# Opening of a fused two-layer kernel: expert mixing as stacked 32-row products, x earlier in the load queue, low rank B split later, int32 conversions regrouped

## The chip, the cores and the metric

The kernel runs on one core of a Trainium2 chip. Its time is the device time of one execution in microseconds (us), lower is better. Engines: PE is TensorE, DVE VectorE, ACT ScalarE, POOL GpSimd, SP the engine that issues most DMAs.

## What is computed

The input x has 64 batches of 32 rows of 512 values, 2048 tokens. Cut to what the change touches:

```python
def cond(x, embedding, W0, b0, W1, b1, W2, b2, weight, bias_k):
    h = gelu(embedding @ W0 + b0)
    h = gelu(h @ W1 + b1)
    att = softmax(h @ W2 + b2)                      # 64 batches x 8 experts
    agg_w = einsum('bk,koi->boi', att, weight)      # a 32x32 matrix for each batch
    agg_b = att @ bias_k                            # 32 values for each batch
    return einsum('boi,bih->boh', agg_w, x) + agg_b[:, :, None]

def qlinear(x, q, scale, A, B):                     # q: integers 0 to 15
    return x @ ((q - 7.5) * (scale * 0.005)[:, None]).T + 0.02 * (x @ A @ B)

def ffn(x):                                         # 512 -> 1376 -> 512
    h = silu(qlinear(x, gate)) * qlinear(x, up)
    return qlinear(h, down)

x = x + ffn(cond(x, ...))
x = x + ffn_fp8(conv_cond(x, ...))
```

## The kernel before, in words

The 2048 tokens go through the first layer in four tiles (t = 0 to 3) of 512 tokens, a tile being four groups of 128. The second layer follows after the last tile. Each engine has one instruction stream of its own, written out in order in a block (`@block.sync`, `@block.tensor`, `@block.scalar`, `@block.gpsimd`, `@block.vector`), and the streams meet by semaphores: an instruction's `then_inc` raises one, `wait_ge` stops the engine until it has a value. A DMA raises its semaphore by 16 when it has landed. What stands behind a wait on an engine's stream stands still with it.

**The opening.** SP (L403 to L440) issues the loads in order: the packed condition inputs, the expert matrices `cond_w`, `bias_k`, the identity, `lr_a`, `lr_b`, slot 0 of the quantised weights, x of tile 0, slots 1 to 3, small scales and masks. PE runs three small layers (L519, L522, L525) with dummy bf16 matmuls between (`keep_clock`, L513; `WARM` says how many at each place). DVE and ACT make the softmax; PE waits for `soft` and for `lr_in` at 2 x 16 (the identity and `lr_a` both raise it) and transposes `att` (L529). DVE copies it as `att_t` (L1026). PE then mixes: eight fp32 products of 8 rows (L535), each 128 x 64, into bank 5, with one dummy matmul in the middle. The bias product `ones.T @ att_bias` has its operand split into an fp32r high part (ACT, L813) and a low part (DVE, L1040) and is two fp32r matmuls (L542, L543); four dummy matmuls follow. ACT (L821) and DVE (L1047) copy the mixed 32 x 32 matrices into the block-diagonal tensor `mix`.

**The condition stage.** `condition(t)` (L553) multiplies x by `mix`, 16 fp32 products of 128 x 128 in a tile, two instructions each. For tile 0 it waits for `mix_ready` and x. DVE adds `agg_b` (L1058), ACT and DVE split the result into an fp32r high part (L826) and a low part (L1068), and PE begins the tile's stream with the low rank products with `lr_a_w` (L681) and the gate and up products (L616).

**Low rank B.** ACT (L816) and POOL (L985) split `lr_b`; SP stores the parts to DRAM (L427), loads slots 4 and 5, loads the parts back in another layout into `lr_b4` (L433), then goes on with further slots. PE first needs `lr_b4` in L626.

**Gate, up and down.** The 1376 hidden units are 11 chunks (ic = 0 to 10) of 128 (the last 96). For each chunk PE makes gate and up (L616, L626), ACT scales (L921, L924), DVE adds the low rank parts (L1245, L1248), ACT applies Silu (L935), DVE multiplies (L1256), ACT and POOL split the product into `h_hi` (L893) and `h_lo` (L995). Then come four down groups j = 0 to 3 (L605), 11 chunks of four matmuls; group 0 of tile 0 waits at each chunk for `h_lo_ready` and for that chunk's converted weights.

**Conversions.** The quantised weights come as int32 in 33 slots of a ring of eight (gate and up of each chunk, then 11 for down). DVE's `convert` (L1053) makes each an fp32r weight; a slot's load waits until the conversion eight before it is done. Six are converted early. In tile 0 each chunk has two, between L1248 and L1256, so slots 6 to 27; the last five (28 to 32) come in a row after the product of chunk 10:

```python
if t == 0:
    for later in range(EARLY + 2 * ic, EARLY + 2 * ic + 2):
        convert(later)
...
if t == 0:
    for later in range(EARLY + 2 * IC, 3 * IC):
        convert(later)
```

## Time and profile before

| | before |
|---|---|
| median of 3 runs | 382.48 us |
| lowest and highest run | 381.16, 382.75 us |
| the profiled execution, its own time | 383.76 us |
| its span, first to last instruction | 382.0 us |
| granted TensorE clock, mean of the span | 0.987 |
| PE busy | 372.2 us, 97% |
| DVE busy | 249.0 us, 65% |
| ACT busy | 172.6 us, 45% |
| POOL busy | 82.3 us, 22% |
| DMA, mean rate | 106 GB/s |

The span is the profiled execution's; the rest of its time lies ahead of the first and behind the last instruction. Start times in all rows count from the first instruction. Matmuls are pipelined, so a row's duration overlaps with the next one's; the pitch is the difference of starts, which the chain of waits shows as the time of each piece. A clock of 1.00 is TensorE's full 2.4 GHz, 0.50 is 1.2 GHz.

### The profile page before, as it was taken

The page shows a single profiled execution, that of the slowest core. Times are in us where ns is not written, and L with a number is a line of the kernel's source. Part 1 is how long each engine was busy: PE and PEld are TensorE (multiplying, and loading weights), DVE is VectorE, ACT ScalarE, POOL GpSimd, SP SyncE. Part 2 cuts the span into 40 slices and gives each one's busy share as a digit, 9 for nine tenths or more (in the row PEclk, how much of TensorE's full clock was granted, in tenths as well). Part 3 has the DMA queues.
Part 4 walks back from the last instruction along what each step waited for, and adds up shares of the span by engine and source line. Part 5 has one row for each costly group of instructions (what it writes and reads, how often), then busy time and mean ns, then how long its engine had stood idle before and what let it go on. Part 6 is the DMA issues. An engine that isn't in the chain of part 4 may idle for free.

```text
span 382.0 us, 5806 instructions
## 1 busy us (share of the span) xinstructions
PE 372.2 (97%) x2233; PEld 307.9 (81%) x2234; DVE 249.0 (65%) x406; ACT 172.6 (45%) x323; POOL 82.3 (22%) x68
## 2 busy tenths in 40 slices
PE   8999999899999999999999999999999999999894
PEld 3877887799888888998888889988888899995341
DVE  2659999826376665263766652638889722797994
ACT  6546798313355554133555541335666510254132
POOL 2101433411123224111233241112332411000000
PEclk9699999999999999999999999999999999999998
DMA  6897575198420000232200002354000399965235
GB/s 208 276 275 238 154 270 161 56 319 184 60 43 0 0 2 0 34 51 42 41 0 3 1 0 33 52 79 112 2 0 2 115 280 233 197 184 92 90 133 222
DMA packets 81964, 40.53 MB, mean 106 GB/s; under 512 B 52344, under 2 KB 72840, under 8 KB 81808
## 3 DMA queue, kind: packets, MB, share of 16 engines
q1 hardware_dynamic: 69280, 37.80, 37.4%
q10 hardware_dynamic: 12480, 1.56, 2.9%
q0 software_dynamic: 176, 0.79, 0.6%
q8 instruction: 18, 0.29, 0.3%
q14 instruction: 10, 0.08, 0.1%
HBM read 26.38 MB, written 13.75 MB: 105 GB/s over the span
## 4 chain that ended last, share of the span: by engine, by line
PE 92%; DVE 5%; issue 1%; DVEq 0%
PE ps L616 41%; PE ps L605 23%; PE ps L626 5%; PE ps L553 4%; PE ps L647 4%; PE ps L784 3%; PE ps L513 2%; PE ps L764 2%; PE ps L681 2%; PE ps L649 2%; DVE down_w L1053 1%; PE ps L568 1%; DVE b_buf L1248 1%; DVE q_fp L1328 1%; PE ps L535 1%
## 5 line engine op out<-in xcount | busy, mean ns | idle before, releaser
L995 POOL TENSOR_TENSOR h_lo<-a_buf,h_hi 128x512 fp32r<-128x512 f32 (+1 forms) x44 | 58.0, 1318 | 125.2 <-ACT h_hi L893 125.2
L605 PE MATMUL ps<-down_w,h_hi 128*128 128x288 f32 (+1 forms) x352 | 76.4, 298 | 1.0 <-DVE down_w L1053 1.0
L605 PE MATMUL ps<-down_w,h_lo 128*128 128x288 f32 (+1 forms) x352 | 74.8, 293 | 0.0
L616 PE MATMUL ps<-x_hi,up_w 128*128 128x512 f32 (+1 forms) x176 | 69.7, 396 | 0.2 <-DVE b_buf L1248 0.2
L616 PE MATMUL ps<-x_hi,gate_w 128*128 128x512 f32 (+1 forms) x176 | 69.9, 397 | 0.0
L616 PE MATMUL ps<-x_lo,gate_w 128*128 128x512 f32 (+1 forms) x176 | 69.4, 395 | 0.0
L616 PE MATMUL ps<-x_lo,up_w 128*128 128x512 f32 (+1 forms) x176 | 69.3, 393 | 0.0
L605 PEld LDWEIGHTS ps<-down_w,h_hi 128*128 128x128 f32 (+1 forms) x352 | 57.2, 189 | 2.6 <-POOL h_lo L995 1.2
L605 PEld LDWEIGHTS ps<-down_w,h_lo 128*128 128x128 f32 (+1 forms) x352 | 56.1, 188 | 0.0
L1256 DVE TENSOR_TENSOR a_buf<-a_buf,b_buf 128x512 f32<-128x512 f32 (+1 forms) x44 | 49.5, 1125 | 9.6 <-ACT a_buf L935 8.5
L921 ACT ACTIVATE a_buf<-ps,gate_sc 128x512 f32<-128x512 f32 (+1 forms) x44 | 30.2, 686 | 27.4 <-POOL h_lo L995 24.8
L1248 DVE TENSOR_TENSOR b_buf<-ps,b_buf 128x512 f32<-128x512 f32 (+1 forms) x44 | 30.2, 686 | 18.9 <-ACT b_buf L924 14.7
L1144 DVE TENSOR_TENSOR y_buf<-ps,y_buf 128x512 f32<-128x512 f32 x16 | 11.1, 691 | 46.7 <-PE ps L568 46.7
L924 ACT ACTIVATE b_buf<-ps,up_sc 128x512 f32<-128x512 f32 (+1 forms) x44 | 30.1, 685 | 23.7 <-PE ps L616 23.6
L1005 POOL TENSOR_TENSOR x_nat<-y_buf,x_nat 128x512 f32<-128x512 f32 x15 | 19.3, 1287 | 95.8 <-DVE y_buf L1144 95.8
L616 PEld LDWEIGHTS ps<-x_hi,up_w 128*128 128x128 f32 (+1 forms) x176 | 32.6, 185 | 8.7 <-DVE b_buf L1248 0.5
L616 PEld LDWEIGHTS ps<-x_lo,up_w 128*128 128x128 f32 (+1 forms) x176 | 32.8, 186 | 8.0
L616 PEld LDWEIGHTS ps<-x_lo,gate_w 128*128 128x128 f32 (+1 forms) x176 | 32.8, 186 | 7.8
L616 PEld LDWEIGHTS ps<-x_hi,gate_w 128*128 128x128 f32 (+1 forms) x176 | 32.6, 185 | 7.9
L1245 DVE TENSOR_TENSOR a_buf<-ps,a_buf 128x512 f32<-128x512 f32 (+1 forms) x44 | 30.3, 688 | 6.6 <-ACT a_buf L921 6.0
L893 ACT ACTIVATE h_hi<-a_buf 128x512 fp32r<-128x512 f32 (+1 forms) x44 | 27.5, 625 | 9.7 <-DVE a_buf L1256 9.7
L935 ACT ACTIVATE a_buf<-a_buf 128x512 f32<-128x512 f32 (+1 forms) x44 | 27.5, 625 | 9.6 <-DVE a_buf L1245 9.3
(179 smaller groups left out, 458.8 us busy)
## 6 DMA issues: line engine op xcount, KB each, us to landing
x_nat<-in_x SPq DMA_DIRECT2D x4, 1024.0 KB, 7.3
out<-x_nat SPq DMA_DIRECT2D x16, 256.0 KB, 2.5
turned<-x_nat SPq DMA_DIRECT2D x12, 256.0 KB, 3.2
x_nat<-in_down_q SPq DMA_DIRECT2D x11, 256.0 KB, 3.1
x_nat<-in_gate_q SPq DMA_DIRECT2D x10, 256.0 KB, 6.2
x_nat<-in_up_q SPq DMA_DIRECT2D x10, 256.0 KB, 8.2
edges<-zeros SPq DMA_DIRECT2D x4, 512.0 KB, 9.2
xt<-turned SPq DMA_DIRECT2D x6, 256.0 KB, 3.4
```

What stands on the lines that cost most here:

```text
L605: last = mm(ps[:, 4 + 2 * (j % 2) + m, 0:HALF + R], part[0:k, ic, j * P:(j + 1) * P], down_w[0:k, ic, m, :], start=first, stop=end)
L616: last = mm(ps[0:k, bank(ic, 2 * m), :], w[:, H * ic + c * k:H * ic + (c + 1) * k], part[:, c, :], start=c == 0 and part is x1_hi, stop=c ...
L626: mm(ps[0:width(ic), bank(ic, 2 * m + 1), :], lr_b4[:, m, ic * P:ic * P + width(ic)], t4[m], start=True, stop=True).then_inc(l_mm, 1)
L893: activation(h_hi[0:k, ic, :], a_buf[0:k, ic % 2, :], copy).then_inc(h_hi_ready, 1)
L921: activation(a_buf[0:k, ic % 2, :], ps[0:k, bank(ic, 0), :], copy, scale=gate_sc[0:k, ic:ic + 1]).then_inc(ag_ready, 1)
L924: activation(b_buf[0:k, ic % 2, :], ps[0:k, bank(ic, 2), :], copy, scale=up_sc[0:k, ic:ic + 1]).then_inc(au_ready, 1)
L935: activation(a_buf[0:k, ic % 2, :], a_buf[0:k, ic % 2, :], ACT.Silu).then_inc(silu_ready, 1)
L995: nc.gpsimd.tensor_tensor(h_lo[0:k, ic, :], a_buf[0:k, ic % 2, :], plain(h_hi[0:k, ic, :]), ALU.subtract).then_inc(h_lo_ready, 1)
L1005: nc.gpsimd.tensor_tensor(x_nat[:, n, :], y_buf[:, j % 2, :], x_nat[:, n, :], ALU.add).then_inc(x2_ready, 1)
L1245: v.tensor_tensor(a, ps[0:k, bank(ic, 1), :], a, ALU.add).then_inc(g_ready, 1)
L1248: v.tensor_tensor(b, ps[0:k, bank(ic, 3), :], b, ALU.add).then_inc(u_ready, 1)
L1256: v.tensor_tensor(a, a, b, ALU.mult).then_inc(h_ready, 1)
```

## The change

- **Mixing.** The expert matrices are loaded four times over, stacked on 32 rows (`cond_w`), beside a second tensor with zeros on rows 0 to 7 and 16 to 23 and the matrices on the others (`cond_w_rest`). DVE makes the fp32r high part of the first, and high times a sign column (+1, -1, +1, -1 by blocks of 8 rows) plus the second: high, low, high, low. The softmax weights are written four times next to two blocks of zeros that POOL clears; two transposes of 32 rows give them four times over, and as two blocks of zeros with two of values. ACT makes the high part from PSUM, DVE the signed sum: high, high, low, low. One fp32r product over 32 rows then has all four partial products; eight take the place of the eight fp32 products and the dummy matmul between them.
- **Bias.** One fp32 product with `ones` and `att_bias` (two instructions) takes the place of the two fp32r products and the splits before them.
- **Loads.** x of tile 0 goes ahead of `lr_a`, `lr_b` and slot 0; `bias_k` behind the identity, with a semaphore of its own.
- **Low rank B.** ACT's high part comes after its copy of `agg_b`, no longer before its copies of `mix`.
- **ACT's Silu table** is loaded after `split_mixed(0)`. **`WARM[4]`** is 2.
- **Conversions.** Chunks 0 to 5 have two, chunks 6 to 10 three (18 to 20, ..., 30 to 32), and those of chunk 10 come after its product.

The diff, without allocations of memory and names of semaphores:

```diff
 BUFS = 3
-WARM = (4, 2, 1, 6, 1)
+WARM = (4, 2, 1, 6, 2)
 LRC = R * I // P
 MIX_BANK, BIAS_BANK = 5, 4
 FIRST_BANK = (6, 3, 7, MIX_BANK)
...
-COND_WIDTHS = (B, P, P, EXPERTS, 1, 1, EXPERTS)
+COND_WIDTHS = (B, P, P, EXPERTS, 1, 1, EXPERTS, 1, 1)
+PARTS = 4
+STACKED = PARTS * EXPERTS
+SPARE = 1856
...
+        pad_gate = sb("pad_gate", [P, 2 * HC * I - 4 * (S // OB) * P], F32, early)
+        cond_w_sb = sb("cond_w_sb", [STACKED, S // OB * P], F32, early)
+        cond_w_left = sb("cond_w_left", [STACKED, S // OB * P], F32, early)
+        cond_w_hi = sb("cond_w_hi", [STACKED, S // OB * P], F32R, early)
+        cond_w_parts = sb("cond_w_parts", [STACKED, S // OB, P], F32R, early)
...
         def _(sp):
             sp.dma_start(cond_in_sb[:], cond_pack).then_inc(cond_in, 16)
-            sp.dma_start(cond_w_sb[:].rearrange("k o p -> k (o p)"), cond_w).then_inc(mixw_in, 16)
-            sp.dma_start(bias_k_sb[:], bias_k).then_inc(mixw_in, 16)
+            sp.dma_start(cond_w_sb[:], cond_w).then_inc(mixw_in, 16)
+            sp.dma_start(cond_w_left[:], cond_w_rest).then_inc(mixw_in, 16)
             sp.dma_start(ident[:], ident_in).then_inc(lr_in, 16)
+            sp.dma_start(bias_k_sb[:], bias_k).then_inc(bias_k_in, 16)
+            sp.dma_start(x_nat[:, 0:TG, :], x_tile(x, 0)).then_inc(x_in[0], 16)
             sp.dma_start(stage_lr_a[:].rearrange("p c m r -> p (c m r)"), lr_a).then_inc(lr_in, 16)
...
             sp.dma_start(stage_lr_b[:].rearrange("p m n -> p (m n)"), lr_b).then_inc(lrb_in, 16)
-            load_slot(0)
-            sp.dma_start(x_nat[:, 0:TG, :], x_tile(x, 0)).then_inc(x_in[0], 16)
-            for n in range(1, 4):
+            for n in range(4):
                 load_slot(n)
             sp.dma_start(gate_sc[:], gate_s).then_inc(scale_in, 16)
             sp.dma_start(up_sc[:], up_s).then_inc(scale_in, 16)
@@ -526,21 +534,21 @@
             keep_clock(WARM[3])
             pe.wait_ge(soft, 4)
             pe.wait_ge(lr_in, 2 * 16)
-            nc.tensor.transpose(ps[0:EXPERTS, 3, 0:B], att[:], ident[0:B, 0:B]).then_inc(att_tr, 1)
+            pe.wait_ge(att_zero, 1)
+            for at, to in ((PARTS // 2, 3), (0, 2)):
+                nc.tensor.transpose(ps[0:STACKED, to, 0:B], att[:, at:at + PARTS, :].rearrange("b n k -> b (n k)"),
+                                    ident[0:B, 0:B]).then_inc(att_tr, 1)
             keep_clock(WARM[4])
 
-            pe.wait_ge(att_ready, 1)
-            pe.wait_ge(mixw_in, 2 * 16)
+            pe.wait_ge(att_parts_ready, 1)
+            pe.wait_ge(mixw_ready, 1)
             for o in range(S // OB):
-                last = mm(ps[:, MIX_BANK, o * B:(o + 1) * B], cond_w_sb[:, o, :], att_t[:], start=True, stop=True)
-                if o == S // OB // 2 - 1:
-                    keep_clock(1)
+                last = mm(ps[:, MIX_BANK, o * B:(o + 1) * B], cond_w_parts[:, o, :], att_parts[:], start=True, stop=True)
             last.then_inc(mix_mm, 1)
 
-            pe.wait_ge(bias_hi, 2)
-            pe.wait_ge(bias_lo, 1)
-            mm(ps[:, BIAS_BANK, :], ones_r[:], att_bias_hi[:], start=True, stop=False)
-            mm(ps[:, BIAS_BANK, :], ones_r[:], att_bias_lo[:], start=False, stop=True).then_inc(aggb_mm, 1)
+            pe.wait_ge(att_ready, 2)
+            mm(ps[:, BIAS_BANK, :], ones[0:EXPERTS, :], att_bias[:].rearrange("k b s -> k (b s)"),
+               start=True, stop=True).then_inc(aggb_mm, 1)
...
@@ -805,15 +813,11 @@
             load_table(1, ACT.Exp)
             act.wait_ge(soft, 2)
             activation(probs[:], logits[:], ACT.Exp, bias=stat[:, 0:1], accum_out=stat[:, 1:2]).then_inc(exp_done, 1)
-            load_table(2, ACT.Silu)
+            act.wait_ge(att_tr, 2)
+            activation(att_hi[:], ps[0:STACKED, 3, 0:B], copy).then_inc(att_hi_ready, 1)
 
             act.wait_ge(lr_in, 2 * 16)
             activation(lr_a_w[:, :, :, 0, :], stage_lr_a[:], copy).then_inc(lra_hi, 1)
-            act.wait_ge(att_ready, 2)
-            activation(att_bias_hi[:], att_bias[:].rearrange("k b s -> k (b s)"), copy).then_inc(bias_hi, 1)
-            activation(ones_r[:], ones[0:EXPERTS, :], copy).then_inc(bias_hi, 1)
-            act.wait_ge(lrb_in, 16)
-            activation(lr_b_parts[:, :, 0, :], stage_lr_b[:], copy).then_inc(lrb_hi, 1)
             act.wait_ge(mix_mm, 1)
             act.wait_ge(mix_zero, 1)
             for q in range(2, OB):
@@ -837,9 +841,12 @@
 
             act.wait_ge(aggb_mm, 1)
             activation(agg_b[:, 0:TILE], ps[:, BIAS_BANK, :], copy).then_inc(aggb_ready, 1)
+            act.wait_ge(lrb_in, 16)
+            activation(lr_b_parts[:, :, 0, :], stage_lr_b[:], copy).then_inc(lrb_hi, 1)
             act.wait_ge(mix_ready, 2)
             activation(mix_kept[:], ps[:, MIX_BANK, :], copy).then_inc(mix_saved, 1)
             split_mixed(0)
+            load_table(2, ACT.Silu)
             act.wait_ge(sel_w_in, 16)
             activation(sel[:], stage_sel[:], copy)
             x_a_high(0)
...
         @block.gpsimd
         def _(pool):
+            nc.gpsimd.memset(att[:, 0:PARTS // 2, :], 0.0).then_inc(att_zero, 1)
             nc.gpsimd.memset(mix[:], 0.0).then_inc(mix_zero, 1)
             nc.gpsimd.memset(zeros[:], 0.0).then_inc(zero_set, 1)
             pool.wait_ge(lrb_hi, 1)
...
             v.memset(warm_ones[:], 1.0).then_inc(const_set, 1)
 
+            dve.wait_ge(mixw_in, 2 * 16)
+            v.tensor_copy(cond_w_hi[:], cond_w_sb[:]).then_inc(mixw_hi, 1)
             dve.wait_ge(cond_in, 16)
+            dve.wait_ge(mixw_hi, 1)
+            v.scalar_tensor_tensor(cond_w_parts[:].rearrange("k o p -> k (o p)"), plain(cond_w_hi[:]), w_sign,
+                                   cond_w_left[:], ALU.mult, ALU.add).then_inc(mixw_ready, 1)
+
             dve.wait_ge(logit_mm, 1)
             v.tensor_tensor(logits[:], ps[0:B, 2, 0:EXPERTS], b2_sb, ALU.add).then_inc(soft, 1)
             dve.wait_ge(soft, 1)
@@ -1021,12 +1035,16 @@
             dve.wait_ge(exp_done, 1)
             v.reciprocal(stat[:, 2:3], stat[:, 1:2]).then_inc(soft, 1)
             dve.wait_ge(soft, 3)
-            v.tensor_scalar(att[:], probs[:], stat[:, 2:3], None, ALU.mult).then_inc(soft, 1)
-            dve.wait_ge(att_tr, 1)
+            v.tensor_scalar(att[:, PARTS // 2:, :], probs[:].unsqueeze(1).to_broadcast([B, PARTS, EXPERTS]),
+                            stat[:, 2:3], None, ALU.mult).then_inc(soft, 1)
+            dve.wait_ge(att_tr, 2)
+            dve.wait_ge(att_hi_ready, 1)
+            v.scalar_tensor_tensor(att_parts[:], plain(att_hi[:]), att_sign, ps[0:STACKED, 2, 0:B], ALU.mult,
+                                   ALU.add).then_inc(att_parts_ready, 1)
             v.tensor_copy(att_t[:], ps[0:EXPERTS, 3, 0:B]).then_inc(att_ready, 1)
 
             dve.wait_ge(att_ready, 1)
-            dve.wait_ge(mixw_in, 2 * 16)
+            dve.wait_ge(bias_k_in, 16)
 
             first = TILE // S
             v.tensor_tensor(att_bias[:], att_t[:, 0:first].unsqueeze(2).to_broadcast([EXPERTS, first, S]),
@@ -1035,10 +1053,6 @@
             dve.wait_ge(lra_hi, 1)
             v.tensor_tensor(lr_a_w[:, :, :, 1, :], stage_lr_a[:], plain(lr_a_w[:, :, :, 0, :]),
                             ALU.subtract).then_inc(lra_ready, 1)
-
-            dve.wait_ge(bias_hi, 1)
-            v.tensor_tensor(att_bias_lo[:], att_bias[:].rearrange("k b s -> k (b s)"), plain(att_bias_hi[:]),
-                            ALU.subtract).then_inc(bias_lo, 1)
 
             dve.wait_ge(mix_mm, 1)
...
+
+            def convert_in_chunk(ic):
+
+                done = [EARLY + 2 * n + max(0, n - IC // 2 - 1) for n in (ic, ic + 1)]
+                for n in range(*done):
+                    convert(n)
...
                     v.tensor_tensor(b, ps[0:k, bank(ic, 3), :], b, ALU.add).then_inc(u_ready, 1)
-                    if t == 0:
-                        for later in range(EARLY + 2 * ic, EARLY + 2 * ic + 2):
-                            convert(later)
+                    if t == 0 and ic < IC - 1:
+                        convert_in_chunk(ic)
                     if t == TILES - 1 and ic == W_SPREAD - 1:
                         largest_of(w_row_mm, bank(W_SPREAD, 1), w_max, w_steps)
                     dve.wait_ge(silu_ready, n + 1)
                     dve.wait_ge(u_ready, n + 1)
                     v.tensor_tensor(a, a, b, ALU.mult).then_inc(h_ready, 1)
+                    if t == 0 and ic == IC - 1:
+                        convert_in_chunk(ic)
...
-                if t == 0:
-                    for later in range(EARLY + 2 * IC, 3 * IC):
-                        convert(later)
                 for j in range(TG):
...
+    def in_parts(values):
+
+        return np.repeat(np.array(values, np.float32), EXPERTS)[:, None]
+
+    cond_w = a(L0_cond_weight).reshape(EXPERTS, S * S)
     lr_a = np.stack([a(L0_ffn_gate_A)[order], a(L0_ffn_up_A)[order]], axis=1).reshape(HC, P, 2 * R).transpose(1, 0, 2)
     cond_pack = np.zeros((P, COND_COLS), np.float32)
     for at, w in zip(COND_AT, (a(cond_128).T, a(L0_cond_W0), a(L0_cond_W1), a(L0_cond_W2), a(L0_cond_b0)[:, None],
-                               a(L0_cond_b1)[:, None], broadcast(L0_cond_b2, B))):
+                               a(L0_cond_b1)[:, None], broadcast(L0_cond_b2, B), in_parts((1, -1, 1, -1)),
+                               in_parts((1, 1, -1, -1)))):
         cond_pack[:w.shape[0], at:at + w.shape[1]] = w
...
-        "cond_w": a(L0_cond_weight).reshape(EXPERTS, S * S), "bias_k": a(L0_cond_bias_k),
+        "cond_w": np.concatenate([cond_w] * PARTS),
+        "cond_w_rest": np.concatenate([np.zeros_like(cond_w), cond_w] * (PARTS // 2)), "bias_k": a(L0_cond_bias_k),
```

## Rows read from the trace of the kernel before

**Rows 1.** The page, engine totals: busy us, share of the span, instructions.

```profile
PE 372.2 (97%) x2233; PEld 307.9 (81%) x2234; DVE 249.0 (65%) x406; ACT 172.6 (45%) x323; POOL 82.3 (22%) x68
```

**Rows 2.** The chain of waits, 0 to 100 us: start, us, what.

```profile
5.94 1.95 PE ps L513 x6
7.89 0.15 PE ps L529
...
8.36 1.08 PE ps L535 x8
...
9.77 1.25 PE ps L535 x8
...
11.98 1.82 PE ps L513 x4
13.80 5.29 PE ps L553 x32
...
31.09 0.38 PE ps L626
...
92.29 4.21 PE ps L605 x32
```

**Rows 3.** Windows: stretch, length, PE busy us, granted clock, DMA share, GB/s.

```profile
12.00:13.80 1.80, 1.80 (x5) 0.50 0.58 185
13.80:19.10 5.30, 5.30 (x33) 0.67 0.86 266
...
88.66:92.23 3.57, 3.57 (x34) 1.00 0.22 63
```

**Rows 4.** Timeline, end of tile 0, DVE and PE: start, us, engine, line, what.

```profile
66.15 0.67 DVE L1248 TENSOR_TENSOR b_buf<-ps,b_buf 128x512 f32<-128x512 f32 x1
...
68.68 0.42 PE L605 MATMUL ps<-down_w,h_hi 128*128 128x288 f32 x2
...
71.76 0.68 DVE L1256 TENSOR_TENSOR a_buf<-a_buf,b_buf 96x512 f32<-96x512 f32 x1
...
72.36 2.85 DVE L1053 TENSOR_SCALAR down_w<-x_nat 128x512 fp32r<-128x512 int32 x5
...
76.17 0.43 PE L605 MATMUL ps<-down_w,h_hi 128*128 128x288 f32 x2
```

**Rows 5.** DMA issues: what, count, KB each, median us from issue to landing.

```profile
stage_lr_a<-in_lr_a SPq DMA_DIRECT2D x1, 128.0 KB, 2.2
...
x_nat<-in_x SPq DMA_DIRECT2D x1, 1024.0 KB, 7.9
...
x_nat<-in_up_q SPq DMA_DIRECT2D x1, 256.0 KB, 8.1
...
lr_b_rows<-lr_b_parts SPq DMA_DIRECT2D x1, 688.0 KB, 3.9
...
lr_b<-lr_b_rows SPq DMA_DIRECT2D x2, 688.0 KB, 7.1
...
x_nat<-in_x SPq DMA_DIRECT2D x1, 1024.0 KB, 6.2
```

**Rows 6.** Timeline of the opening, SP's queue, DVE and POOL.

```profile
3.75 0.43 SPq L416 DMA_DIRECT2D x_nat<-in_x  x1
...
8.32 0.68 DVE L1032 TENSOR_TENSOR att_bias<-att_t,bias_k_sb 8x512 f32<-8x512 f32 x1
...
9.16 0.42 DVE L1036 TENSOR_TENSOR lr_a_w<-stage_lr_a,lr_a_w 128x256 fp32r<-128x256 f32 x1 [0.15 <-ACT lr_a_w L811]
...
10.61 1.64 POOL L985 TENSOR_TENSOR lr_b_parts<-stage_lr_b,lr_b_parts 128x688 fp32r<-128x688 f32 x1 [7.93 <-ACT lr_b_parts L816]
...
11.05 1.75 DVE L1047 COPY mix<-ps 32x32 f32<-32x32 f32 x8 [0.67 <-PE ps L535]
```

**Rows 7.** Timeline, tile 0, POOL and DVE where they meet.

```profile
39.31 1.29 POOL L995 TENSOR_TENSOR h_lo<-a_buf,h_hi 128x512 fp32r<-128x512 f32 x1 [3.06 <-ACT h_hi L893]
...
39.79 1.36 DVE L1256 TENSOR_TENSOR a_buf<-a_buf,b_buf 128x512 f32<-128x512 f32 x1 [0.44 <-ACT a_buf L935]
```

More of the change, by code:

```diff
@@ L68, in width, with build @@
     return min(P, I - ic * P)
-def build(nc, x, cond_pack, cond_w, bias_k, gate_q, up_q, gate_s, up_s,
+def build(nc, x, cond_pack, cond_w, cond_w_rest, bias_k, gate_q, up_q, gate_s, up_s,
           lr_a, lr_b, down_q, down_s, down_a, down_b, conv_w, ctx_w, fside, ffn_w,
@@ L125, in build @@
         early = ExitStack()
-        pad_gate = sb("pad_gate", [P, 2 * HC * I], F32, early)
+        pad_gate = sb("pad_gate", [P, 2 * HC * I - 4 * (S // OB) * P], F32, early)
[3 more added lines that the diff above has]
+        cond_w_parts = sb("cond_w_parts", [STACKED, S // OB, P], F32R, early)
         cond_in_sb = sb("cond_in_sb", [P, COND_COLS], F32, early)
@@ L131, in build @@
         probs = sb("probs", [B, EXPERTS], F32, early)
-        att = sb("att", [B, EXPERTS], F32, early)
+        att = sb("att", [B, PARTS + PARTS // 2, EXPERTS], F32, early)
+        att_hi = sb("att_hi", [STACKED, B], F32R, early)
+        att_parts = sb("att_parts", [STACKED, B], F32R, early)
         att_t = sb("att_t", [EXPERTS, B], F32, early)
@@ L145, in build @@
         stage_ctx_w = sb("stage_ctx_w", [P, S], F32, early)
[L147 removed]
+        used = 4 * (COND_COLS + 2 * B + (2 + PARTS * 3 // 2) * EXPERTS + 3 * B + 6 + S + TILE + SPARE + HC * 2 * R + P
                     + GROUPS + P + S + S)
@@ L156, in build @@
         early.close()
-        cond_sb, w0_sb, w1_sb, w2_sb, b0_sb, b1_sb, b2_sb = (
+        cond_sb, w0_sb, w1_sb, w2_sb, b0_sb, b1_sb, b2_sb, w_sign, att_sign = (
             cond_in_sb[0:rows, COND_AT[n]:COND_AT[n] + COND_WIDTHS[n]]
-            for n, rows in enumerate((P, P, P, P, P, P, B)))
+            for n, rows in enumerate((P, P, P, P, P, P, B, STACKED, STACKED)))
         phase2 = ExitStack()
```

10 lines of the change are left out of this document (4 added, 6 removed).

## The prediction, made before the changed kernel ran

> **What bounds the kernel now.** I began with the page's engine totals: TensorE (PE) is busy for 372.2 of 382.0 us, so a saving must come from a stretch where PE waits, runs at the lower clock or does work that can be cut [rows 1]. The chain of waits of the first 60 us says what PE does there. At 7.89 it transposes the softmax weights, from 8.36 it mixes the expert matrices in eight fp32 products (L535, two instructions each) until 9.77 + 1.25 = 11.02, then come the two bias products (L542, L543, 0.96 us) and at 11.98 four clock-keeping matmuls (L513), and from 13.80 the first condition stage (L553, 32 instructions, 5.29 us); at 19.1 the long L681/L616 stream begins [rows 2]. No step of it is a DMA. The windows give the clock: 0.50 in 12.00 to 13.80, a mean of 0.67 in the condition stage, and the same 32 instructions take 3.57 us at clock 1.00 in the second token tile [rows 3]. So 0.50 is the 1.2 GHz level and 1.00 is the 2.4 GHz level, and the low stretch costs L553 alone 5.29 - 3.57 = 1.7 us. PE had run little but small products before the fall: L535, whose operands fill 8 rows. The other weak place is the first down product: PE starts L605 at 68.68 and its second j group at 76.17, 7.49 us for 44 instructions; at the pitch of the later ones (4.21 us for 32 in the chain, 0.132 each) these need 5.8 us. 1.65 us are therefore waits, on the last product (71.76), what is split from it, and the five conversions that DVE does in a row from 72.36 [rows 4].
>
> I name T the start of the transpose, 7.9 now, and measure the opening from it.
>
> **The change, part by part.**
>
> *SP queue: when T can come.* PE waits ahead of the transpose for lr_in at 32, that is for ident and for lr_a, and the change leaves this wait. Before, lr_a stood ahead of x, was issued some 1.4 us before it and took 2.2 us to land, so it was in at about 4.5, long before T; x was issued at 3.75 and took 7.9 us (11.65) [rows 5, 6]. Now x (1 MB) stands between ident and lr_a. SP is occupied 0.43 us by an issue [rows 6]: cond_pack 0.74, cond_w 1.19, the rest 1.6, ident 2.0, bias_k 2.4, x 2.75, lr_a 3.2. The x load of tile 2, which had the queue to itself, took 6.2 us [rows 5]; so x lands between 2.75 + 6.2 = 8.95 and 2.75 + 7.9 = 10.65. I take 9.3, near the low end, since only 0.3 MB more of small loads are ahead of it, and no quantised slot. The loads that followed x before did not overtake it: the 256 KB slot issued next, at about 4.2, took 8.1 us and landed at 12.3, 0.65 after x [rows 5]. lr_a, half as large, then lands some 0.6 after x. T moves to 9.9: **+2.0 us**, bounds 9.5 and 11.2. The Trainium skill (DMA: Bandwidth & Descriptors, Queues, rings and completion order) says that each DMA engine consumes one queue's descriptors in ring order; the landings agree. By that rule alone no part of lr_a starts before the same engine's part of x.
>
> *DVE ahead of the logits.* New there: a 32x1024 copy to fp32r and a 32x1024 scalar_tensor_tensor. The nearest rows are 512-wide: a conversion (2.85/5 = 0.57 [rows 4]) and a two-operand operation (0.68 [rows 6]); doubled, 1.1 + 1.3 = 2.4 us. Their input, two loads of 128 KB just behind the first one, I put at 4.0, so they end at 6.4. The logits left PE at 5.94 [rows 2]: 0 to 0.6 us on the softmax chain. Cost nothing, because PE waits for lr_a anyway; without that cover 0.4. The wider att (64x32) adds under 0.1, with the same cover.
>
> *From T to the first condition matmul.* Two transposes, ACT's att_hi, DVE's att_parts, each 0.3, with two clock-keeping matmuls beside them (before, transpose and copy took 0.5 until L535): PE starts mixing at T + 1.2. The mixing goes from 16 instructions and a clock-keeping one (2.66 us) to 8 of one pass. Their pitch is not in the trace: below, 0.03 us, if 64 columns go as the 288 of L605 do (0.132); above, 0.156, the second half of L535 (1.25/8). A weight load of 128 columns stands before each as in L535, so I take 0.14 near the upper end, 1.1 us: T + 2.3. The bias goes from two fp32r to two fp32 instructions of 512 columns: 4 times the 128 columns of L553, whose instruction takes 3.57/32 = 0.11 us at the high clock, so 0.9 us, and 1.7 at the low one, against 0.96 before. That is T + 4.0, and the four matmuls of keep_clock (1.82 us at the low clock) end at T + 5.8. DVE's side is shorter: att_parts until T + 0.95, att_t 0.3, att_bias 0.68, lr_a low 0.42, then the mix cells 1.75 [rows 6] give T + 4.1, hidden behind PE at the low clock. Before it was 13.8 - 7.9 = 5.9. Saving **-0.1**: what the mixing gives back goes to the longer way into it and the fp32 bias. The 32 condition instructions then start at 9.9 + 5.8 = 15.7 instead of 13.8.
>
> *The clock in the condition stage.* Of 13.80 to 19.10 about 3.5 us were at 0.50 [rows 3]: (1 - 0.67)/0.5 x 5.3. If the clock rises at the same moment (17.3), the stage has 1.6 us at half rate, 0.8 us of its 3.57, and 2.8 at the full one, 4.4 in all: -0.9. If it rises later by as much as the work is later: 0. I take -0.8. x is in at 9.3, and hides. **Opening: +2.0 - 0.1 - 0.8 = +1.1 us.**
>
> *lr_b split later.* POOL's low half of lr_b started at 10.61, right after ACT's high half, and took 1.64; SP then stored it, from 12.3 [rows 6]. The high half now follows the agg_b copy, which ends at about T + 4.7 = 14.6: 0.8 more, POOL from 15.4, the store at 17.1, 4.8 later. SP's queue behind that wait: the store, slots 4 and 5, the two lr_b loads, slots 6 and 7, the down and conv inputs and slots 8 to 11. Store and loads took 3.9 and 7.1 us (a median of two; the second some 1 us more) [rows 5], so lr_b was laid at about 12.3 + 3.9 + 1 + 8 = 25 and is now at 29 to 30, while PE asks for it at 31.1 + 1.1 [rows 2]. The slots have the same slack of 2 us or more before their product. 0, bounds 0 and +1. ACT's Silu table load now lies under PE's first L681/L616 products, where no one waits for ACT: 0.
>
> *Conversions spread.* Chunks 6 to 9 get three conversions instead of two, chunk 10 none before its product and three after. One more adds at most 2.85/5 = 0.57 to DVE; I take 0.35, as a group waits for POOL once, however long it is. Four of them make 1.4 by chunk 10 if DVE has no idle time in these chunks, 0.7 if half is absorbed, which I take. PE waits for u of chunk 9 before L605: that came at 66.15 + 0.67 = 66.8, L605 started at 68.68, 1.9 later [rows 4]: covered. Last product: before at 71.76, after two conversions; now about 71.0, where POOL's h_lo of chunk 9 runs until about 71.7. The row for such a meeting is L1256 at 39.79: 1.36 us instead of 0.68, until POOL's h_lo from 39.31 was over [rows 7]. So product 10 ends 72.35, ACT's h_hi 73.0, POOL's h_lo 74.4 to 74.7, conversions by 74.7. Unstalled, PE needs them at 68.7 + 40 x 0.132 = 74.0. Waits left 0.4 to 0.7, and I take 0.4: **-1.25 us**, bounds -0.6 and -1.65. The Trainium skill (SBUF — State Buffer, Who interferes with whom) has it that a DVE operation with both inputs in SBUF and a GpSimd one that reads there block each other; the 1.36 agrees. By the rule without a meeting the saving would be 1.65.
>
> **Sum.** The profiled execution took 383.76 us. +1.1 - 1.25 = -0.15: 383.6. It stands 1.28 above the median of the runs (382.48), so the forecast is **382.3 us**. A measurement of this kernel can't tell less than about 0.5%, 1.9 us, from no change.
>
> **The rivals.**
> 1. *lr_a does not wait for x, and the clock holds* (0.15). T is 8.0 to 8.3, PE is not idle, mixing and bias run at 1.00 and end at T + 2.6; DVE's mix cells bind, T + 4.1; condition from 12.5 to 16.1, 3.0 before 19.1. With the conversions -4.25: 378.2. For it: lr_a is small. Against: the landings behind x. If only T is early and the clock falls all the same, condition starts at 8.0 + 5.8: -1.25 alone, 381.2, no change (0.12).
> 2. *T is late, but the clock stays high or is back at once* (0.10). Condition from 14.3 to 17.9, -1.2, in all -2.45: 380.0.
> 3. *Slower: the clock stays low through the whole condition stage* (0.16). PE has nothing from 7.9, where its six clock-keeping matmuls end, to T. Then come products of 32 and of 8 rows, as weak as those ahead of the fall now. The stage, from 15.7 at half rate, takes 7.1 us, until 22.8: +3.7 - 1.25 = +2.45, 384.9. It decides if the rise comes after about 21.5. The Trainium skill (TensorE: Matmul & The Clock Gate, What's actually happening) calls the throttled clock the default, released by activity. That bears for this rival; the row agrees in that the clock fell among the small products.
> 4. *The spread conversions give little* (0.09). If DVE's third conversion waits on POOL too, product 10 is later by up to 1 us and only 0.3 is saved: 383.3.
> The forecast has 0.38.
>
> **The numbers.** Faster takes rivals 1 (0.15) and 2 (0.10) and a little of the forecast's low end: 0.27. Slower takes rival 3 and the top of T (11.2, +1.3) with rival 4: 0.18. Same 0.55. The range leaves out most of rival 1 and the upper half of rival 3: 379.4 to 384.9; the forecast's own bounds are 381 to 384.
>
> **What would show it.** The transpose near 9.9 with lr_a's landing before it, and PE idle from 8 on; x in by 9.3; mixing 0.5 to 1.1 us; the bias product 0.9 or 1.7; condition near 15.7; the L681 stream near 20.2; and 6.1 us from the first L605 to the second j group. A transpose at 8 or a granted clock of 1.00 up to the condition stage makes the forecast wrong.

## The result, and the profile after

The changed kernel takes 384.05 us (median of 22 runs, 381.99 to 386.15), the kernel before 382.42 in the 22 runs beside it (381.14 to 383.87). The ratio is 1.0038, with a 95% interval of 1.0025 to 1.0052: slower by about 1.5 us. The forecast was 382.3 us and no change that a measurement can tell. The time is inside the forecast's range (379.4 to 384.9), but the change is clear of the noise, and slower had been given 0.18.

The profiled execution of the changed kernel took 384.64 us, with a span of 382.8, 0.8 us longer than before. From the page, the engine totals:

```profile
PE 370.3 (97%) x2227; PEld 306.2 (80%) x2227; DVE 249.1 (65%) x408; ACT 172.3 (45%) x322; POOL 82.0 (21%) x69
```

PE is busy for 1.9 us less than in [rows 1], in a span 0.8 us longer: it waits 2.7 us more. Where, the chain of waits says. Start, us, what; the layers, the transposes and the condition stage have new line numbers (keep_clock is L521 now, the transposes L539, mixing L546, bias L550, the condition stage L561, the first product of a group L689, lr_b's product L634, the down product L613).

```profile
7.51 0.24 DVE att L1038
7.75 2.66 issue
10.42 0.28 PE ps L539 x2
...
11.36 1.70 PE ps L546 x8
13.06 1.87 PE ps L550 x2
14.93 1.82 PE ps L521 x4
16.74 4.45 PE ps L561 x32
...
33.19 0.37 PE ps L634
...
72.97 1.29 DVE a_buf L1275
...
74.28 0.65 ACT h_hi L900
...
74.99 1.42 POOL h_lo L1003
...
76.46 2.90 PE ps L613 x20
...
89.56 3.57 PE ps L561 x32
```

Against [rows 2] this is the whole balance. The transpose comes at 10.42 instead of 7.89 (+2.5), with 2.66 us ahead of it that are put down to nothing ("issue"). The condition stage starts at 16.74 instead of 13.80 (+2.9) and ends at 21.19 instead of 19.09 (+2.1). That 2.1 is still there at lr_b's product (33.19 for 31.09). At the condition stage of the second tile it has shrunk to 0.9 (89.56 for 88.66), so the end of tile 0 gave 1.2 back.

What ended the 2.66 us isn't named in the chain. The DMA issues, with the median us from issue to landing in the last column, and the timeline of the opening give it:

```profile
x_nat<-in_x SPq DMA_DIRECT2D x1, 1024.0 KB, 7.0
stage_lr_a<-in_lr_a SPq DMA_DIRECT2D x1, 128.0 KB, 6.9
```

```profile
3.00 0.41 SPq L416 DMA_DIRECT2D x_nat<-in_x  x1
3.45 0.50 SPq L417 DMA_DIRECT2D stage_lr_a<-in_lr_a  x1
...
4.53 0.68 DVE L1025 CAST cond_w_hi<-cond_w_sb 32x1024 fp32r<-32x1024 f32 x1 [2.97 <-DMA cond_w_left<-in_cond_w_rest]
...
5.32 1.27 DVE L1028 SCALAR_TENSOR_TENSOR cond_w_parts<-cond_w_hi,cond_in_sb,cond_w_left 32x1024 fp32r<-32x1024 f32 x1
...
10.42 0.27 PE L539 MATMUL ps<-ident,att 64*32 64x64 f32 x2 [3.28 <-issue]
```

x was issued at 3.00 and landed 7.0 later, at 10.0; lr_a at 3.45 and 6.9 later, at 10.35. PE transposes 0.07 after that. Before, lr_a landed 2.2 us after its issue [rows 5].

The granted clock in the condition stage and in the bias product with the clock-keeping matmuls ahead of it (stretch, length, PE busy us and instructions, granted clock, DMA share, GB/s):

```profile
16.74:21.19 4.45, 4.45 (x34) 0.81 0.50 151
...
12.88:16.54 3.66, 3.66 (x8) 0.50 0.03 7
```

The first two steps from the transpose on, all engines (us, then PE, PEld, DVE, ACT, POOL busy, and the granted clock):

```profile
10.42:11.36 0.94, 0.80 (x4) 0.20 (x4) 0.32 (x2) 0.52 (x2) 0.00 (x0) 1.00 1.02 393
11.36:13.06 1.70, 1.70 (x9) 1.70 (x10) 1.09 (x3) 0.00 (x0) 0.00 (x0) 0.58 0.72 190
```

So PE's clock was still at the high level when it came back from its idle stretch, and fell to 1.2 GHz about 0.3 us into the mixing (1.70 us at a mean of 0.58). It was back (0.81 over 4.45 us) at about 18.4. Before, it rose at about 17.3 [rows 3].

Not every step of this is a property of the kernel. e3 below has the same opening, and in its profiled execution x landed at 9.7 and `lr_a` at 9.9. The chain of waits of e3:

```profile
7.93 2.10 issue
10.03 0.28 PE ps L539 x2
...
10.97 1.08 PE ps L546 x8
12.04 1.55 PE ps L550 x2
13.60 1.82 PE ps L521 x4
15.42 5.37 PE ps L561 x32
```

Here the mixing ran at the high clock (1.08 us) and the condition stage at the low one for longer (5.37). From the transpose to the end of the stage it is 10.76 us, and 10.77 in the changed kernel (10.42 to 21.19), against 11.20 before (7.89 to 19.09). The low stretch fell on other steps, and the sum is the same: what the two executions share is a late transpose and 0.4 us less behind it.

### The profile page after: what moved, and what is told of

It is laid out like the page before. It is cut to its first block, busy times and chain, and to the rows that moved or that the text cites. A ratio compares the mean times of both kernels' runs of the same rounds, so it can differ in the third digit from the quotient of the medians.

```text
span 382.8 us, 5796 instructions
## 1 busy us (share of the span) xinstructions
PE 370.3 (97%) x2227; PEld 306.2 (80%) x2227; DVE 249.1 (65%) x408; ACT 172.3 (45%) x322; POOL 82.0 (21%) x69
## 4 chain that ended last, share of the span: by engine, by line
PE 91%; DVE 4%; issue 2%; ACT 1%; POOL 0%; DVEq 0%
PE ps L624 41%; PE ps L613 23%; PE ps L634 5%; PE ps L561 4%; PE ps L655 4%; PE ps L792 3%; PE ps L772 2%; PE ps L689 2%; PE ps L657 2%; PE ps L521 1%; PE ps L576 1%; DVE a_buf L1275 1%; DVE q_fp L1346 1%; PE ps L713 1%; DVE b_buf L1268 1%
## 5 line engine op out<-in xcount | busy, mean ns | idle before, releaser
L613 PE MATMUL ps<-down_w,h_hi 128*128 128x288 f32 (+1 forms) x352 | 76.3, 298 | 0.2 <-POOL h_lo L1003 0.2
L613 PE MATMUL ps<-down_w,h_lo 128*128 128x288 f32 (+1 forms) x352 | 74.8, 293 | 0.0
L613 PEld LDWEIGHTS ps<-down_w,h_hi 128*128 128x128 f32 (+1 forms) x352 | 57.2, 189 | 1.5 <-POOL h_lo L1003 0.5
L1275 DVE TENSOR_TENSOR a_buf<-a_buf,b_buf 128x512 f32<-128x512 f32 (+1 forms) x44 | 50.6, 1150 | 9.3 <-ACT a_buf L942 8.0
L613 PEld LDWEIGHTS ps<-down_w,h_lo 128*128 128x128 f32 (+1 forms) x352 | 56.1, 188 | 0.0
```

What stands on the lines that cost most here:

```text
L613: last = mm(ps[:, 4 + 2 * (j % 2) + m, 0:HALF + R], part[0:k, ic, j * P:(j + 1) * P], down_w[0:k, ic, m, :], start=first, stop=end)
L1275: v.tensor_tensor(a, a, b, ALU.mult).then_inc(h_ready, 1)
```

## The experiments

Ratios are to the kernel before, on the same chip, from 12 runs if nothing else is said, with 95% intervals. The first four ask what the opening and the conversions are worth apart.

**e1: lr_a issued ahead of x, all else as in the changed kernel.**

```diff
-            sp.dma_start(x_nat[:, 0:TG, :], x_tile(x, 0)).then_inc(x_in[0], 16)
             sp.dma_start(stage_lr_a[:].rearrange("p c m r -> p (c m r)"), lr_a).then_inc(lr_in, 16)
+            sp.dma_start(x_nat[:, 0:TG, :], x_tile(x, 0)).then_inc(x_in[0], 16)
```

> The changed kernel with lr_a issued ahead of x, both still early. Theory: the transpose waits for lr_a, which landed only behind x (10.32 us); with lr_a ahead it lands near 5.2, the transpose starts at 7.9 instead of 10.42, the mixing runs at the high clock, and the condition stage starts 2.5 to 3.5 us sooner than the changed kernel's 16.74. Time 2 to 3.5 us below the changed kernel's 384.05, ratio to before 0.994 to 0.998. Rival, that the way into the stacked products and the fp32 bias are what costs: the transpose moves, but the condition stage starts after 15.7 and the ratio stays above 1.001.

Measured: 0.9952 (0.9935 to 0.9968), 381.10 us: by the ratios 0.86% below the changed kernel, 3.3 us (2.95 by the medians), by the swap of two lines. The timeline of PE shows the transpose at 7.86:

```profile
7.86 0.28 PE L539 MATMUL ps<-ident,att 64*32 64x64 f32 x2 [0.57 <-DVE att L1038]
...
8.81 1.07 PE L546 MATMUL ps<-att_parts,cond_w_parts 32*128 32x64 f32 x8
9.73 1.10 PE L550 MATMUL ps<-att_bias,ones 8*128 8x512 f32 x2
...
11.81 5.46 PE L561 MATMUL ps<-mix,x_nat 128*128 128x128 f32 x32
17.03 0.47 PE L689 MATMUL ps<-x_hi,lr_a_w 128*128 128x512 f32 x1
```

Mixing and bias ran at the high clock; the clock fell only in the condition stage (0.67 from 11.81 to 17.03). The long stream starts 3.9 us earlier than in the changed kernel (17.03 for 20.95 in the timelines of PE). Not all of it reaches the end, since something new is late. The chain of e1:

```profile
13.12 1.65 POOL lr_b_parts L993
...
14.85 3.95 DMA lr_b_rows<-lr_b_parts
...
19.58 9.95 DMA lr_b<-lr_b_rows
...
29.57 0.52 PE ps L634
```

PE now waits for lr_b, whose split the change had moved back.

**e2: x at its old place, behind lr_b and the first slot, all else changed.**

```diff
-            sp.dma_start(x_nat[:, 0:TG, :], x_tile(x, 0)).then_inc(x_in[0], 16)
...
-            for n in range(4):
+            load_slot(0)
+            sp.dma_start(x_nat[:, 0:TG, :], x_tile(x, 0)).then_inc(x_in[0], 16)
+            for n in range(1, 4):
```

> The changed kernel with x of tile 0 back behind lr_b and slot 0. Theory: x lands at about 11.8 and the condition stage asks for it near 13.5, so x is in time and this gives what e1 gives, within 0.5 us. Rival, that x sooner is worth something once lr_a is out of the way: the first condition matmul waits for x, and the time is 0.5 to 2 us above e1.

Measured: 0.9978 (0.9957 to 1.0000), 381.59 us. PE transposed at 8.09 and started the condition stage at 12.07, 0.1 after x was in, without a wait for it. So loading x sooner isn't shown to be worth anything: e1 has x sooner and is at 381.10, 0.5 us lower, and the two intervals overlap. The 0.2 us by which this transpose is later than e1's is DVE's: its two new operations ended at 6.89 and the logits stood behind them.

**e3: the old grouping of the conversions, all else changed.** **e4: the kernel before with the spread conversions alone.**

```diff
-                    if t == 0 and ic < IC - 1:
-                        convert_in_chunk(ic)
+                    if t == 0:
+                        for later in range(EARLY + 2 * ic, EARLY + 2 * ic + 2):
+                            convert(later)
...
+                if t == 0:
+                    for later in range(EARLY + 2 * IC, 3 * IC):
+                        convert(later)
```

(e3; e4 is the reverse of it, in the kernel before.)

> The changed kernel with the conversions grouped as before. Theory: the spread conversions save about 1.2 us (the opening lost 2.1 us in the profiled executions and the second condition stage is only 0.9 later), so this is 1.2 slower than the changed kernel, ratio to before 1.007. Rival, that they save nothing and the 1.2 came from elsewhere: ratio 1.004 as the changed kernel.

> The kernel before with only the conversions spread. Theory: the waits in the first down group of tile 0 fall from 1.65 to about 0.4 us; 1.2 us faster, ratio 0.9965 to 0.9975. Rival: POOL's h_lo of the last chunk comes no sooner and at most 0.4 us is saved, ratio 0.999 to 1.000.

Measured: e3 1.0076 (1.0051 to 1.0100), 385.38 us; e4 0.9961 (0.9942 to 0.9980), 381.40. The conversions give 0.4% either way, 1.2 to 1.5 us, and all the rest of the change, the opening, costs 0.76%, 2.8 us by the medians (385.38 for 382.57). The two parts add up: 0.9961 x 1.0076 = 1.0037. The timeline of DVE in e4 shows the step:

```profile
69.36 1.28 DVE L1261 TENSOR_TENSOR a_buf<-a_buf,b_buf 96x512 f32<-96x512 f32 x1
70.56 1.08 DVE L1053 TENSOR_SCALAR down_w<-x_nat 128x512 fp32r<-128x512 int32 x3
```

Three conversions are left behind the last product where there were five, and that product takes 1.28 instead of 0.68, since it meets POOL's h_lo.

**e5: the kernel before with x ahead of lr_a, and nothing else.** It asks whether the order alone costs, without 32-row products.

```diff
+            sp.dma_start(x_nat[:, 0:TG, :], x_tile(x, 0)).then_inc(x_in[0], 16)
             sp.dma_start(stage_lr_a[:].rearrange("p c m r -> p (c m r)"), lr_a).then_inc(lr_in, 16)
...
-            load_slot(0)
-            sp.dma_start(x_nat[:, 0:TG, :], x_tile(x, 0)).then_inc(x_in[0], 16)
-            for n in range(1, 4):
+            for n in range(4):
```

> The kernel before with only x of tile 0 issued ahead of lr_a, nothing else of the change. Theory: the transpose waits for lr_a behind x, so it starts at 9.5 to 10.5 instead of 7.9 and the time is 1.5 to 3 us above before, ratio 1.004 to 1.008. Rival, that the new mixing route or the bias lost the time: ratio 0.998 to 1.001.

Measured: 1.0021 (1.0005 to 1.0037), 383.32 us, below what was expected. In this kernel the profile names the releaser, in PE's timeline:

```profile
8.42 0.21 PE L528 MATMUL ps<-ident,att 64*8 64x64 f32 x1 [1.16 <-DMA stage_lr_a<-in_lr_a]
```

lr_a was issued 0.6 us earlier than in the changed kernel (2.81) and took 5.5 us instead of 6.9: the transpose is late by 0.5, not by 2.5. So the order costs what the landing makes of it. In the changed kernel 224 KB more stand ahead of x (cond_w has 128 KB instead of 32, and cond_w_rest 128). That this makes the difference isn't shown: in the profiled executions of the changed kernel, e3, e7, e8 and e12, which issue these loads alike, lr_a took 6.9, 6.5, 6.1, 5.6 and 6.7 us, so the landing moves by over 1 us from one execution to the next. Nor does e5's profiled execution show where its 0.6 us goes: its condition stage started at 13.32, before the 13.80 of the kernel before, since the clock fell later.

**e8: the changed kernel, with a semaphore of its own for ident.** x stays first; only the transpose no longer waits for lr_a, which it doesn't read.

```diff
-            sp.dma_start(ident[:], ident_in).then_inc(lr_in, 16)
+            sp.dma_start(ident[:], ident_in).then_inc(ident_here, 16)
...
-            pe.wait_ge(lr_in, 2 * 16)
+            pe.wait_ge(ident_here, 16)
...
-            act.wait_ge(lr_in, 2 * 16)
+            act.wait_ge(ident_here, 16)
+            act.wait_ge(lr_in, 16)
```

> The changed kernel, x still ahead of lr_a, but ident raises a semaphore of its own and the transpose waits for that alone. Theory: the transpose starts at 7.9; ACT and DVE now wait for lr_a (10.3) ahead of the mix copies, so these start near 10.8 to 11.3, 0.9 later than in e1 and 2 before the changed kernel: 1.5 to 3 us below the changed kernel, ratio to before 0.996 to 0.9995. Rival, that the order of the loads matters by itself: no better than 1.003.

Measured: 0.9974 (0.9956 to 0.9992), 381.68 us: 0.64% below the changed kernel. This shows that the wait and not the traffic is the cost: the loads are issued in the same order, the transpose came at 7.77. e8 stays behind e1 in the median, but the intervals overlap. In the profiled execution the next thing late was the split of x. The timelines of POOL and of DVE and PE around it:

```profile
13.04 1.66 POOL L995 TENSOR_TENSOR lr_b_parts<-stage_lr_b,lr_b_parts 128x688 fp32r<-128x688 f32 x1 [10.31 <-ACT lr_b_parts L847]
```

```profile
13.60 1.38 DVE L1069 TENSOR_SCALAR gate_w<-x_nat 128x512 fp32r<-128x512 int32 x1
...
16.32 0.47 PE L690 MATMUL ps<-x_hi,lr_a_w 128*128 128x512 f32 x1 [0.76 <-DVE x_lo L1084]
```

A conversion took 1.38 us instead of some 0.4 to 0.6 and ended just behind POOL's low half of lr_b (14.98 and 14.70), and x_lo behind it was late.

**e7 and e12: more clock-keeping matmuls while PE waits**, 18 and 11 instead of 6.

```diff
-WARM = (4, 2, 1, 6, 2)
+WARM = (4, 2, 1, 18, 2)
```

(e7; e12 has 11.)

> The changed kernel, load order as it is, with 18 instead of 6 clock-keeping matmuls in PE's wait for lr_a (12 more at 0.21 us, 2.6 us). Theory: the clock fell because PE stood still; filled, the low stretch comes later and is shorter (one of 3.4 instead of 6.8 us), mixing takes about 1.1 instead of 1.7 us, the transpose stays at 10 to 10.5; 1 to 2 us below the changed kernel, ratio to before 0.999 to 1.001. Rival: the clock falls anyway from the small products behind, ratio 1.003 to 1.004 as the changed kernel.

> The changed kernel with 11 instead of 6 clock-keeping matmuls ahead of the transpose (1.1 us more at the high clock, 2.1 at the low one; in e7 the 18 ran past lr_a's landing). Theory: they end at 8.6 to 10.2, before lr_a lands, so the transpose is not later, the clock stays low for less of the opening (mean granted clock above 0.988), and the time is 0.5 to 1.5 us below the changed kernel, ratio to before 1.000 to 1.0025. Rival, that the clock fell from the small products alone: mean clock 0.988, ratio 1.003 to 1.005.

Measured: e7 1.0024 (1.0008 to 1.0040), 383.67 us; e12 1.0016 (1.0000 to 1.0032), 383.06. They are 0.14% and 0.22% below the changed kernel, and the intervals overlap with its own: whether filling the gap gives anything back isn't settled. e12's chain has 0.395 us for each of 11 matmuls, so most of them ran at the low level:

```profile
6.14 4.35 PE ps L521 x11
...
13.39 1.82 PE ps L521 x4
15.21 4.35 PE ps L561 x32
```

The clock fell all the same, later (0.50 from 13.39). The matmuls also held the transpose: lr_a was in at 10.1, and the 11 ended at 10.49. In e7 lr_a was in at 9.6, and the 18 (5.75 us) ended at 11.77. What the clock gained was partly lost to that, and PE then waited for lr_b, as in e1. The granted clocks of all runs point to the idle stretch: the mean is 0.989 or less in 16 of the 22 runs of the changed kernel, in 2 of 12 of e12 and in none of the 12 each of e7, e8 and e1, where PE has no such idle stretch. But e9, which has none either, shows it in 5 of 12.

**e6 and e11 (the same kernel twice): lr_a and lr_b ahead of x, and lr_b's high half split before the mix copies.** The theory: with the transpose on time, lr_b is the next to be late, so both small loads go first.

```diff
-            sp.dma_start(x_nat[:, 0:TG, :], x_tile(x, 0)).then_inc(x_in[0], 16)
             sp.dma_start(stage_lr_a[:].rearrange("p c m r -> p (c m r)"), lr_a).then_inc(lr_in, 16)
...
             sp.dma_start(stage_lr_b[:].rearrange("p m n -> p (m n)"), lr_b).then_inc(lrb_in, 16)
+            sp.dma_start(x_nat[:, 0:TG, :], x_tile(x, 0)).then_inc(x_in[0], 16)
...
             activation(lr_a_w[:, :, :, 0, :], stage_lr_a[:], copy).then_inc(lra_hi, 1)
+            act.wait_ge(lrb_in, 16)
+            activation(lr_b_parts[:, :, 0, :], stage_lr_b[:], copy).then_inc(lrb_hi, 1)
...
             activation(agg_b[:, 0:TILE], ps[:, BIAS_BANK, :], copy).then_inc(aggb_ready, 1)
-            act.wait_ge(lrb_in, 16)
-            activation(lr_b_parts[:, :, 0, :], stage_lr_b[:], copy).then_inc(lrb_hi, 1)
```

> The changed kernel with loads in the order ident, bias_k, lr_a, lr_b, x, slots, and ACT's high half of lr_b back ahead of its mix copies. In e1 PE waited about 0.5 us for the lr_b load from DRAM. Theory: that wait goes, L634 starts with the products ahead of it near 28.6 to 29.1 instead of 29.6, and the time is 0.3 to 0.8 us below e1, ratio to before 0.993 to 0.9945. Rival: the lr_b split delays ACT's mix copies by as much as it saves, ratio 0.995 to 0.997.

> e6 again, beside e9 and e10: ratio 0.993 to 0.9945 if e6 held; what it is below e4's 0.9961 is what the new opening is worth once neither lr_a nor lr_b is late, 0.5 to 1 us. Rival: the opening is worth nothing and e6 was luck, 0.996.

Measured: 0.9934 (0.9916 to 0.9951), 380.33 us from 6 runs, and 0.9947 (0.9928 to 0.9967), 380.61 from 7. This is the lowest time measured, below both kernels. But the conversions alone (e4) are at 0.9961 (0.9942 to 0.9980) and the swap alone (e1) at 0.9952 (0.9935 to 0.9968), and both intervals overlap with these two. So neither the stacked mixing with its new opening nor the early lr_b is shown to gain anything over the conversions; 0.1 to 0.3% is open. PE's timeline in e11:

```profile
7.77 0.28 PE L539 MATMUL ps<-ident,att 64*32 64x64 f32 x2
...
11.74 3.84 PE L561 MATMUL ps<-mix,x_nat 128*128 128x128 f32 x32
15.37 0.47 PE L689 MATMUL ps<-x_hi,lr_a_w 128*128 128x512 f32 x1
```

The stream starts near 15.6, 5.6 us before the changed kernel's, without a wait for lr_b.

**e9: e4 with lr_b split late.** It prices the late split in a kernel whose transpose is on time.

```diff
-            act.wait_ge(lrb_in, 16)
-            activation(lr_b_parts[:, :, 0, :], stage_lr_b[:], copy).then_inc(lrb_hi, 1)
...
             activation(agg_b[:, 0:TILE], ps[:, BIAS_BANK, :], copy).then_inc(aggb_ready, 1)
+            act.wait_ge(lrb_in, 16)
+            activation(lr_b_parts[:, :, 0, :], stage_lr_b[:], copy).then_inc(lrb_hi, 1)
```

> The kernel of e4 (before, conversions spread) with ACT's high half of lr_b moved behind its agg_b copy, as in the change. Theory: the store to DRAM starts 2.5 us later, the lr_b load lands at 28 to 29.5, and PE's first L626 (29.6 in e4) is just reached: 0 to 0.5 us above e4, ratio to before 0.996 to 0.9975. Rival, that the slots queued behind it hold up the conversions too: 1 us or more above e4, ratio above 0.9985.

Measured: 0.9981 (0.9967 to 0.9996), 381.89 us, against 381.40 of e4: +0.5 us, with overlapping intervals (it lies between the theory and the rival). The profiled execution had no wait at lr_b's product (31.05 there), so a cost in the others isn't shown.

**e10: e6 with the old fp32r bias product and its splits.**

```diff
-            pe.wait_ge(att_ready, 2)
-            mm(ps[:, BIAS_BANK, :], ones[0:EXPERTS, :], att_bias[:].rearrange("k b s -> k (b s)"),
-               start=True, stop=True).then_inc(aggb_mm, 1)
+            pe.wait_ge(bias_hi, 2)
+            pe.wait_ge(bias_lo, 1)
+            mm(ps[:, BIAS_BANK, :], ones_r[:], att_bias_hi[:], start=True, stop=False)
+            mm(ps[:, BIAS_BANK, :], ones_r[:], att_bias_lo[:], start=False, stop=True).then_inc(aggb_mm, 1)
...
+            act.wait_ge(att_ready, 2)
+            activation(att_bias_hi[:], att_bias[:].rearrange("k b s -> k (b s)"), copy).then_inc(bias_hi, 1)
+            activation(ones_r[:], ones[0:EXPERTS, :], copy).then_inc(bias_hi, 1)
...
```

> The kernel of e6 with the bias product as before: high and low part split on ACT and DVE, two fp32r matmuls. Theory: at the high clock the fp32 bias (0.94 us in e6) hides behind the mix copies, so does this one, but its splits (ACT 0.63 + 0.29, DVE 0.68) stand ahead of those copies, which start 0.4 to 0.8 us later: ratio 0.3 to 0.8 us above e6, 0.994 to 0.996. Rival, that the fp32 product costs more than the splits: 0.3 us or more below e6.

Measured: 0.9992 (0.9976 to 1.0009), 382.42 us, 1.8 above e11, which ran beside it, and above what was expected. PE's timeline:

```profile
12.11 0.46 PE L555 MATMUL ps<-att_bias_hi,ones_r 8*128 8x512 f32 x1 [0.92 <-DVE att_bias_lo L1066]
...
14.04 5.26 PE L566 MATMUL ps<-mix,x_nat 128*128 128x128 f32 x32 [0.27 <-ACT mix L835]
```

PE waits 0.92 us for the low half of the bias, but what holds the condition stage is ACT: it makes the splits first and begins to copy mix cells at 12.14. In e6, whose transpose came at about the same time (8.68 and 8.80), it began at 11.10, and the stage at 12.99 instead of 14.04. On PE the fp32 product is the dearer one, 0.94 us at the high clock against 0.63 for the two fp32r ones (12.11 to 12.74); it pays since it needs no splits. So about 1 us of the 1.8 is seen. Where the rest comes from isn't shown: in the profiled executions the stage itself took 5.26 us here and 3.84 in e6, as the clock fell in the one and not in the other.

## Why the prediction was wrong, point by point

**The bound, and the direction of the opening: right.** PE is the bound, the gap came where it was named, and its cause is the wait for lr_a behind x: e1 and e8 take it away by two different edits and both gain.

**T: +2.0 forecast, +2.5 measured.** x landed at 10.0, not 9.3, and lr_a 0.35 behind it, not 0.6. x took 7.0 us from issue, between the two rows I had (6.2 and 7.9), and I had chosen near the low end. SP issued both 0.25 later than I put it. The 0.5 is of this execution: lr_a landed at 9.0 in e8, 9.6 in e7, 9.9 in e3 and 10.1 in e12, and the forecast's 9.9 lies among them, as 10.42 lies inside its bounds (9.5 and 11.2).

**DVE ahead of the logits: right.** The copy took 0.68 us, not 1.1, the operation 1.27 (1.3 forecast); they ended at 6.6 (6.4). att was ready at 7.75, as before, since ACT's table load ran until 6.70 beside them. The cover named was lr_a; there was a second one. It doesn't always suffice: in e2 the two operations ended at 6.89, the logits came right behind them, and att was ready at 8.05.

**From T to the condition stage: -0.1 forecast, +0.4 measured** (10.42 to 16.74 is 6.3, against 5.9). The way into the mixing was 0.94 instead of 1.2, the bias 1.87 instead of 1.7, keep_clock 1.82 as forecast. What was off is the mixing: 1.70 us instead of 1.1. At the high clock 1.1 is right (1.07 in e1); here the clock had fallen (0.58), a pitch of 0.21 that I had not taken, since I had put mixing at the high level and the bias at the low one. Counted from T, the fall was placed at 2.3 and came at about 1.2. I also set the fp32 bias (0.9 or 1.7 us, by the clock) against the 0.96 that the two fp32r products took before; that was at the low clock, and at the high one they take 0.63 (e10). So the new bias product costs PE more at either level (1.87 here, 0.94 in e11).

**The clock in the condition stage: -0.8 forecast, -0.84 measured** (4.45 for 5.29), and for the wrong reason. I let the clock rise at the same moment as before, 17.3; it rose at about 18.4. The stage also started 1.0 later than forecast, and the two errors cancel here. That is luck: in e3's profiled execution the stage took 5.37, and nothing of the 0.8 was saved.

**The opening: +1.1 forecast, +2.1 measured in the profiled executions, +2.8 in the medians of the runs. This is the step that failed: the sum +2.0 - 0.1 - 0.8 was mis-sized, not its mechanism.** In the profiled execution the 1.0 is the T term (0.5) and the low pitch of the mixing and the bias (0.6 + 0.2, less 0.3 of the way in). Behind the transpose the terms -0.1 and -0.8 promised 0.9 us back; both executions with this opening, the changed kernel's and e3's, gave 0.4 (10.77 us for 11.20 from the transpose to the end of the condition stage). And the runs of e3 against those of the kernel before put the whole opening at 2.8 us, more than the profiled executions show. A likely reason is that the profiled one of the kernel before ran at a low clock, 0.987, where the median of its runs is 0.995.

**lr_b and the slots: right for this kernel**, no wait at L634 (33.19 is 31.09 + 2.1). But the cover is thin: PE's weight loads wait 0.7 us for it in e1 and 0.6 in e7, whose transpose is late too; in the changed kernel the condition stage ended only at 21.19, against 17.27 in e1, so PE asked for lr_b later.

**The conversions: -1.25 forecast, -1.2 measured** by the chain, -0.4% by e3 and e4. From the first down product to the second group it took 6.33 us (70.76 to 77.09), 7.49 before and 6.1 forecast. The last product ran from 72.97 to 74.26, stretched by POOL's h_lo (72.41 to 73.70). The chain follows it through h_hi to h_lo at 76.41, so the bound was this chain of three, not the conversions, which were in at 75.25.

**The sum against the median.** Against the profiled execution before, the forecast was 383.6, and the profiled execution after took 384.64: 1.0 off, which is what the opening was off in that execution. In the medians it is 1.75 off (384.05 for 382.3). The other 0.7 is the way I came from one to the other. I took off 1.28, what the profiled execution of before stood above its median. But that execution had a mean clock of 0.987, and the runs of the kernel before at that clock take 383.8 in the median; at 0.995 they take 382.3, at 0.999 381.1 (35 runs beside e1). The term "-0.8 for the clock" is a gain against such an execution, which an average one has less of to give. The changed kernel stood only 0.6 above its own median when profiled, at 0.988. Its runs go the same way: 382.0 to 382.5 at 0.992, 383.5 to 384.9 at 0.987 to 0.989, 385.4 to 386.2 at 0.984 and 0.985. (One of 385.6 at 0.997 falls out of this, and three of e3, 386.2 to 387.2 at 0.996 to 1.000; that the record doesn't show all low time, see the last section, may be why.) Its median clock is 0.9885, that of the kernel before in the runs beside e1 0.995.

**The rivals.** Rival 1 is refuted by the landing at 10.35. e1 makes its premise true, and its time is 381.1, not 378.2: in its profiled execution the clock fell all the same in the condition stage (its variant, at 381.2) and lr_b is next. Rival 3, slower, had the right sign and half of the mechanism: the clock was low longer on useful work, but it was back inside the condition stage. Rival 2 is refuted by the 0.58 in the mixing, rival 4 by e3 and e4. That the lower clock of the changed kernel's runs comes from PE's idle 2.7 us is made likely by e7 and e12, not shown: with the idle stretch filled the median clock is 0.994 and 0.993, against 0.9885, but the record leaves out a slow start (last section), and e7's profiled execution has one, 5.75 us for 18 matmuls. The kernel before has runs at 0.987 without any idle stretch. What the idle stretch costs in time by way of the clock stays open too: e7 and e12 gain only 0.1 to 0.2%, within their intervals.

## What to carry to other kernels

A small load that the first steps wait for goes ahead of a large one in the same queue; and a semaphore that counts two loads makes every waiter wait for the later of them, so give the one that is read first its own. When a wait in the opening is removed, price the next operand in line at once (lr_b here). And try the parts of a change one by one: the conversions alone gave 0.4%, and the best opening on top of them 0.1 to 0.3% more, which isn't settled, while the opening as it was bundled with them cost 0.76%. Before a profiled execution is used as the base of a sum, look where its granted clock stands among the runs: here 0.012 of the mean clock was 2.7 us, more than the whole change.
